# A fourth PSUM bank for two attention streams, taken from a third, and every engine's order laid out anew

## The reference

```
x = x + latent_attention(LN(x))      # low-rank keys/values, rotation of 16-wide heads, softmax
x = x + head_mixing(LN(x), ctx)      # per token, 16 heads of width 64 attend to the 16 heads of ctx
x = x + routed_ffn(LN(x))            # the 128 best tokens go through gelu(h W1 + b1) W2 + b2
x = x + sparse_attention(LN(x))      # of each row of scores the 25 largest are kept, the others set to 0, softmax
x = x + context_attention(LN(x), ctx, lens)   # keys past a sample's length are masked
x = x + linear(LN(x), ternary(weight))
```

## Time and profile before

| | |
|---|---|
| time, median of 3 runs | 6425.71 us (6419.53 to 6441.65) |
| the profiled execution's own time | 6419.66 us |
| its span, first to last instruction | 6417.9 us |
| busy share PE, PEld, DVE, ACT, POOL | 89%, 59%, 70%, 62%, 23% |
| mean granted TensorE clock | 0.914 of full |
| matmul records | 37476 |
| a double pass in the loop | 382.2 us for most |

### The profile page before, as it was taken

How to read it: one execution, slowest core, us unless ns; L and a number is a source line. 1 busy time by engine, 2 the same in 40 slices (tenths; PEclk the granted TensorE clock), 3 DMA queues, 4 the chain that set the end, 5 groups by cost and what they waited for, 6 DMA issues and landing times. The chain is left out here.

```text
span 6417.9 us, 109223 instructions
## 1 busy us (share of the span) xinstructions
PE 5732.7 (89%) x37476; PEld 3762.5 (59%) x37762; DVE 4510.0 (70%) x16186; ACT 4001.4 (62%) x9761; POOL 1506.5 (23%) x2564
## 2 busy tenths in 40 slices
PE   6799899899998999899899998999899899998875
PEld 3566566566556666556566555666556566556542
DVE  1476777677776677777677776777787767777763
ACT  2566666666676666676666676666676656676642
POOL 0122222122222222222222222222222222222220
PEclk7898999999999999999989999999999989999975
DMA  2000000000000000000000000000000000000000
GB/s 83 4 3 8 8 8 6 6 8 5 8 6 10 4 8 4 8 8 6 6 8 5 8 6 10 4 8 4 8 8 6 10 4 5 8 6 8 4 4 4
DMA packets 29373, 53.28 MB, mean 8 GB/s; under 512 B 8146, under 2 KB 9811, under 8 KB 27987
## 3 DMA queue, kind: packets, MB, share of 16 engines
q1 hardware_dynamic: 28770, 45.73, 2.2%
HBM read 37.33 MB, written 8.39 MB: 7 GB/s over the span
## 5 line engine op out<-in xcount | busy, mean ns | idle before, releaser
L972 POOL TENSOR_TENSOR t_pr<-t_pr,sc 128x512 f32<-128x512 f32 x512 | 650.6, 1271 | 1554.3 <-ACT t_pr L896 1553.8
L404 DVE TENSOR_REDUCE m_nm<-bankM 128x2 f32<-128x512 f32 x1024 | 669.0, 682 | 454.9 <-PE bankM L394 454.6
L945 DVE MATCH_REPLACE8 wk<-m,wk 128x256 f32<-128x256 f32 x2048 | 819.8, 407 | 0.0
L941 DVE MAX8 m<-wk 128x8 f32<-128x256 f32 x2048 | 756.3, 410 | 0.0
L448 PE MATMUL bankM<-m_q,m_kT 32*128 32x512 f32 x2048 | 685.6, 750 | 0.0
L394 PE MATMUL bankM<-m_kT,m_q 32*128 32x256 f32 x4096 | 613.7, 419 | 35.5 <-DVE m_nm L404 28.2
L902 ACT ACTIVATE t_pr<-t_pr,t_nm 128x256 f32<-128x256 f32 x1024 | 463.8, 502 | 264.5 <-POOL t_pr L972 260.3
L707 ACT ACTIVATE xk_area<-bankH,xb 64x256 f32<-64x256 f32 x1024 | 479.3, 468 | 125.5 <-PE bankH L602 106.9
L462 ACT ACTIVATE m_pT<-bankM,keymask 128x512 f32<-128x512 f32 x512 | 323.7, 683 | 314.6 <-PE bankM L448 313.9
L966 POOL TENSOR_SCALAR mx<-m 128x2 f32<-128x2 f32 x512 | 115.4, 225 | 1705.9 <-DVE wk L945 1702.9
L394 PEld LDWEIGHTS bankM<-m_kT,m_q 32*128 32x128 f32 x4096 | 369.4, 193 | 230.1 <-issue 145.7
(11 more groups left out here) (207 smaller groups left out, 11627.9 us busy)
## 6 DMA issues: line engine op xcount, KB each, us to landing
xin<-x_in SPq DMA_DIRECT2D x32, 256.0 KB, 2.7
ctxA<-ctx_in SPq DMA_DIRECT2D x32, 256.0 KB, 2.9
ctxB<-ctx_in SPq DMA_DIRECT2D x32, 256.0 KB, 2.7
out<-x SPq DMA_DIRECT2D x32, 256.0 KB, 2.0
w<-w_w SPq DMA_DIRECT2D x2, 1024.0 KB
xwq<-w_xwq SPq DMA_DIRECT2D x1, 1024.0 KB
xwk<-w_xwk SPq DMA_DIRECT2D x1, 1024.0 KB
xwv<-w_xwv SPq DMA_DIRECT2D x1, 1024.0 KB
```

What stands on the lines that cost most here:

```text
L404: nc.vector.tensor_reduce(b["nm"][:, i % 2, 2 * (i // 2) + x, :], banks[u % 3][:].rearrange("p (j s) -> p j s", j=2), AX.X, ALU.max, negat ...
L941: link.inc(nc.vector.max(top, src[:, t, :]))
L945: m = nc.vector.match_replace(out=wk[:, k, t, :], in_to_replace=take, in_values=src[:, t, :], imm_value=-BIG)
L972: nc.gpsimd.tensor_tensor(sp_[:, u % 2], taken[:, u % 2], sc[:, u % 3], ALU.mult).then_inc(g["sp_mul"], 1)
```

## The change

bankM gets four banks and bankH two.

- Score steps of m and c go through four banks (2i and 2i+1 mod 4), and step i waits for max 2i-2; steps 0 and 1 do not wait for a max. The maxima read bank u mod 4.
- Transposed score steps go through bankM 0, 1 and 3 in turns of one bank instead of two: step i waits for 2i-1 exps instead of 2i (step 1 for one).
- Stream h has one list TURNS of its 17 early steps (12 projections, LN transposes, four value transposes), which take turns on the two banks, each waiting for the eviction two turns back. By the list all four query projections fall on bank 1, the LN and value transposes on 0 and 1: v0 0, v1 1, v2 0, ln 1, v3 0, q0 1, t0 0, q1 1, t1 0, q2 1, t2 0, q3 1, t3 0, k0 1, k1 0, k2 1, k3 0.
- All quad scores use bankH 0, and quad s waits for the exps of quad s-1 (before: s-2). Bank 1 has what bank 2 had. FFN steps are renumbered alike; the second layer's first four steps wait for four gelus at once.
- Both tables are new for all four engines. The number of loop rounds stays 14.

No instruction of a compute engine is added or taken away.

```diff
-        bankT, bankM, bankH = banks("bankT", 2), banks("bankM", 3), banks("bankH", 3)
+        bankT, bankM, bankH = banks("bankT", 2), banks("bankM", 4), banks("bankH", 2)
...
         def at_scores_T(pe, n, b, bank, i):
             m, c = i // 2, i % 2
+            bank = [bank[(0, 1, 3)[(2 * i + x) % 3]] for x in range(2)]
             yield
             if i == 0:
                 pe.wait_ge(*at(g[n + "_m3"], 1))
+            elif i >= 2:
+                pe.wait_ge(*at(g[n + "_ex"], 2 * i - 1))
             else:
-                pe.wait_ge(*at(g[n + "_ex"], 2 * i))
+                pe.wait_ge(*at(g[n + "_ex"], 1))
...
-                else:
-                    pe.wait_ge(*at(g[n + "_nm"], max(1, 2 * i - 1)))
-                at_scores(n, b, [bankM[2 * i % 3], bankM[(2 * i + 1) % 3]], i, masked)
+                elif i >= 2:
+                    pe.wait_ge(*at(g[n + "_nm"], 2 * i - 2))
+                at_scores(n, b, [bankM[2 * i % 4], bankM[(2 * i + 1) % 4]], i, masked)
...
+        TURNS = ["v0", "v1", "v2", "ln", "v3", "q0", "t0", "q1", "t1", "q2", "t2", "q3", "t3", "k0", "k1", "k2", "k3"]
+            for n, what in enumerate(TURNS):
+                bank = bankH[n % 2]
+                yield
...
+                if n >= 2:
+                    pe.wait_ge(*at(*turn_read(n - 2)))
...
                 if s < QUADS:
                     yield
                     if s == 0:
                         pe.wait_ge(*at(g["hm_ev"], 48))
-                    if s >= 2:
-                        pe.wait_ge(*at(g["hm_ex"], 4 * (s - 1)))
+                    if s >= 1:
+                        pe.wait_ge(*at(g["hm_ex"], 4 * s))
                     for i in range(4):
                         c = 4 * s + i
-                        last = nc.tensor.matmul(bankH[s % 2][:, i * P:(i + 1) * P], xqT[:, c, :], xkT[:, c, :], start=True, stop=True)
+                        last = nc.tensor.matmul(bankH[0][:, i * P:(i + 1) * P], xqT[:, c, :], xkT[:, c, :], start=True, stop=True)
...
             for f in range(FF // P):
                 yield
-                pe.wait_ge(*at(g["md_hid"], f + 1))
+                pe.wait_ge(*at(g["md_hid"], max(4, f + 1)))
```

More of the change, by code:

```diff
@@ L97 @@
+        t7 h t c3 h m t2 m h t4 h2 t6 m t2 h t h c t4 h t5 h t"""),
 }
@@ L588, in tensor_h @@
         def tensor_h(pe):
-            for k in range(12):
-                which, quad = k // 4, k % 4
+            for n, what in enumerate(TURNS):
+                bank = bankH[n % 2]
                 yield
-                if k == 0:
+                if n == 0:
                     past(pe, "md_x3", "ctxA_in")
[L594 to L599, removed]
-                    for d in range(ND):
[L601 to L612, removed]
@@ new lines, in tensor_h @@
+                if n >= 2:
+                    pe.wait_ge(*at(*turn_read(n - 2)))
+                if what == "ln":
+                    pe.wait_ge(*at(g["ln1_xn"], 2))
+                    for d in range(ND):
+                        for t in range(NT):
+                            last = nc.tensor.transpose(bank[:, d * S + t * P:d * S + (t + 1) * P],
+                                                       lnH["xn"][:, t, d * P:(d + 1) * P], w["ident"][:])
+                    last.then_inc(g["ln1_tr"], 1)
+                elif what[0] == "t":
+                    v = int(what[1])
+                    if v == 0:
+                        pe.wait_ge(*at(g["hm_ev"], 16))
@@ L613, in tensor_h @@
                     for i in range(8):
-                        last = nc.tensor.transpose(bankH[2][:, i * XD:(i + 1) * XD], xvT[:, v * 8 + i, :], w["ident"][0:XD, 0:XD])
+                        last = nc.tensor.transpose(bank[:, i * XD:(i + 1) * XD], xvT[:, v * 8 + i, :], w["ident"][0:XD, 0:XD])
                     last.then_inc(g["hm_vtr"], 1)
+                else:
+                    quad = int(what[1])
+                    if what == "q0":
+                        pe.wait_ge(*at(g["ln1_xT"], 1))
+                    wt, src = {"v": ("xwv", ctxA), "q": ("xwq", lnH["xT"]), "k": ("xwk", ctxA)}[what[0]]
+                    for hp in range(2):
+                        for d in range(ND):
+                            c = (quad * 2 + hp) * P
+                            last = nc.tensor.matmul(bank[:, hp * S:(hp + 1) * S], w[wt][:, d, c:c + P], src[:, d, :],
+                                                    start=(d == 0), stop=(d == ND - 1))
+                    last.then_inc(g["hm_proj"], 1)
@@ L659, in tensor_h @@
             for d in range(ND):
-                last = nc.tensor.matmul(bankH[2][:, 0:S], w["wrt"][:, d, :], lnH["xT"][:, d, :], start=(d == 0), stop=(d == ND - 1))
+                last = nc.tensor.matmul(bankH[0][:, 0:S], w["wrt"][:, d, :], lnH["xT"][:, d, :], start=(d == 0), stop=(d == ND - 1))
             last.then_inc(g["md_sps"], 1)
@@ L669, in tensor_h @@
             for t in range(NT):
-                last = nc.tensor.transpose(bankH[1][:, t * P:(t + 1) * P], pick[:, t, :], w["ident"][:])
+                last = nc.tensor.transpose(bankH[0][:, t * P:(t + 1) * P], pick[:, t, :], w["ident"][:])
             last.then_inc(g["md_ptr"], 1)
@@ L691, in tensor_h @@
             for t in range(NT):
-                last = nc.tensor.matmul(bankH[2][:, t * D:(t + 1) * D], pickT[:, t, :], yff[:], start=True, stop=True)
+                last = nc.tensor.matmul(bankH[0][:, t * D:(t + 1) * D], pickT[:, t, :], yff[:], start=True, stop=True)
             last.then_inc(g["md_u"], 1)
```

102 lines of the change are left out of this document (54 added, 48 removed).

## The result

The changed kernel took 6501.2 us (median of 4 runs, 6471.0 to 6538.7), the kernel before on the same chip 6422.6: ratio 1.0126 [1.0069, 1.0182]. A second set of 7 runs on another chip gave 6542.0 us and 1.0191 [1.0157, 1.0224]. The forecast was 6305 us in a range of 6215 to 6465, with a chance of 0.23 for slower.

A forecast was written before the change was run, and what follows sets the result against it. PE was taken to bound the loop, losing time to waits and half-clock stretches. From 6419.7 us, -20 (end passes), -35 (loop waits) and -60 (clock) gave 6305 us; own range 6270 to 6340, range of all cases 6215 to 6465.

The forecast's parts named there:

- Fourth bank, ends: Single-stream first and last pass and the four between: M's bank waits go, together -20 us, bounds -8 and -35.
- deducted 3 us: Four passes between the ends: 6 us gained from the fourth M bank, less 3 for the tighter h.
- my slower rival: Single quad bank: each lap's seven quad waits for the previous exps 0.5 us late, +105 us, 6470 us; chance 0.23.
- Loop waits: Per double pass: 8.7 us of waits removed, 6.4 added, net -2.3; -35 us over about 15 double passes.
- The choice: Lap's end: token choice after t's last round, and gelu's start behind m.onT, add 1.7 us per lap, 3.4 per double pass.
- h.s0 in lap 2: PE's wait for key evictions ahead of h's first quad in lap 2: 2.8 us where it was 2.1.
- LN5: c's LN5 follows a t round and a quad maximum on DVE: +0.8 us per lap, 1.6 per double pass.
- t.tr3, 0.75 us: Lap 1: about 0.75 us of wait ahead of this t transpose, its exps behind two key evictions on ACT.
- Clock: Lap 1's 20.5 us fall stays away in about half of the double passes: 7.5 x 8 = -60 us.
- nothing like 3.5 us idle in 10.5: Walk through lap 1: largest waits 0.75, 0.5 and 0.45 us, so its clock fall, 8 us, may not come.
- The rule that I set aside: Bank waits themselves feed the clock falls, so removing them should help in both laps: -120 us in place of -60.
- What the forecast named as fatal: Forecast wrong if mean clock stays at 0.914, or PE waits several us for the token choice at each lap's end.

The follow-up runs named there:

- Experiments 4: Kernel before with four idle matmuls each behind the shift-row and h.s0 waits: 6579.1 us, 1.021; one more ahead of m's score steps 1 and 2: 0.9779.
- 6: t's second and third selection rounds over half the columns: kernel before 0.9801, with idle matmuls 0.9587; changed kernel 0.992, with them 0.9723, or with t earlier instead 1.0091.
- Experiments 2: Changed kernel with h's token choice on VectorE moved behind the first round of t's last head, not its last round: 6525.6 us, 1.0176.

## Why the forecast failed, by its steps

- **Fourth bank, ends: -20 forecast, -8 measured (1053 to 1045), of which -3 in the single pass, which the forecast had counted with the loop.** The bank waits went nearly as said, and the low clock fell with them, for which I had counted nothing (by 7 us in the first pass and by 19 in the last): first pass 114.0 to 104.4 us, last 102.5 to 87.3. But the pass with m and h alone went from 134.4 to 154.3, for which I had deducted 3 us: PE is idle 34.8 us there instead of 24.8, and the low clock is 69 instead of 38. There no t or c covers the two-bank H. Of its waits (PE's in that pass, changed kernel) the last is the one that my slower rival described (0.6 us before); the other two are turns on the two banks by transposes of probabilities (3.7 before) and by projections (none before):

```profile
PE bankH L646 <- ACT xot L756: 6.8, 4, 1.7
...
PE bankH L633 <- ACT xq_area L727: 5.0, 4, 1.4
PE bankH L656 <- ACT xp L749: 4.6, 2, 2.3
```

- **Loop waits: -2.3 forecast, +7.4 and +7.9 of idle time and +4 to 5 us of length measured.** Removed were 5.4 and not 8.7: exps went from 4.5 to 2.8, maxima from 1.2 to 0.4, and the copies of shift rows and layer norm from 4.4 to 1.5. Added were some 12 and not 6.4. The choice was sized about right (3.7 against 3.4), and h.s0 in lap 2 came out at 2.7 (forecast 2.8); LN5 was oversized (the waits for layer norms grew by 0.4, forecast 1.6). The failed term is t: I had followed one transpose (t.tr3, 0.75 us) and not the others, and six of them wait for 5.9 us in all and six value steps for 3.0.
- **Clock: -60 forecast, +74 and -18 in the two profiles (63.4 and 48.8 us of low clock against 51.7, at 0.45 over 14 passes).** With the waits this step turned the sign. Long falls did go, from 1.93 per double pass to 1.29 and 0.86, but those of lap 2 (13 to 6 and 5), not those of lap 1 (10 to 12 and 7), which I had named; the 4 behind m's score steps went too. Yet with the waits that the order adds come short falls (which wait goes with which fall isn't shown), 1.4 per pass before and 5.4 to 6.2 now, mostly of 3.4 to 6.8 us, and the falls left in lap 1 last up to 30.7 us instead of up to 20.5. I had weighed each wait by its length, looked for the few of over 1 us, and taken "nothing like 3.5 us idle in 10.5" for safety.
- **The rule that I set aside.** The Trainium skill, "TensorE: Matmul & The Clock Gate", section "A second HAM failure mode: psum-queue depth-cycling", tells of a kernel whose short idle gaps between groups of matmuls, while it cycles through PSUM banks, made the clock swing. I held against it that bank waits of 0.6 in m's phase are followed by no fall. That was read from one pass and is wrong for the trace as a whole: 4 of the 27 long falls of before, of 27.3 us each, begin right behind m's waits for maxima of 0.2 and 0.4 us. One of them (PE in order of time, then the stretches before the fall and in it):

```profile
2065.35 1.13 PE L394 MATMUL bankM<-m_kT,m_q 32*128 32x256 f32 x8 [0.18 <-DVE m_nm L404]
2066.41 1.16 PE L636 MATMUL bankH<-xk_area,xq_area 72*128 72x128 f32 x8
2067.99 1.54 PE L394 MATMUL bankM<-m_kT,m_q 32*128 32x256 f32 x8 [0.41 <-DVE m_nm L404]
...
2058.10:2068.60 10.50, 9.72 (x67) 6.92 (x67) 10.50 (x41) 7.93 (x18) 3.45 (x5) 1.00 0.10 28
2068.60:2095.90 27.30, 26.66 (x130) 17.01 (x127) 18.92 (x59) 9.46 (x28) 5.99 (x13) 0.50 0.00 1
```

Experiments 4 and 6 agree with the page: without m's bank waits of 0.2 to 0.5 us, 26 long falls in 14 passes went in the one and 7 in the other. But the same waits were followed by no long fall in 24 of 28 laps of before, so by themselves they do not bring one.

- **The slower rival, 0.23.** The sign was its own, the place was not: in the loop no quad waits for its predecessor's exps. What the forecast named as fatal did occur: the clock did not rise from 0.914, and PE waits for the choice at each lap's end, 2.6 and 1.6 us. Experiments 2 and 6 show that this wait alone was not the loss.
- Left open: why the same program position falls in some passes and not in others (those of one execution differ by 82 us of low clock), and which of the order's steps makes t's transposes late.

## What to carry to other kernels

Where the granted clock has low stretches, read the length of each loop pass against its low-clock time first; the slope (here 0.45) prices the clock apart from the waits. Then look at the thin phases in which TensorE pauses often and briefly, and try a few idle matmuls there, one place at a time: ten per lap gave 3.7% here, most fills elsewhere gave nothing or cost. Count falls over all passes and not in one, and compare executions of equal mean clock: two profiles of the same changed kernel lie 76 us apart. And when an order is planned afresh, list every wait it adds, small ones too, on the stream that was not the subject of the change.

## What the hardware showed that I had not expected

- The same instructions, with PE idle for nearly the same time (40.0 and 38.0 us), ran a double pass in 375 and in 406 us in one execution.
- Idle time ahead of a fall does not rank places: 3.5 us in 10.5, 1.5 in 10.5 and 1.0 in 9.5 were each followed by 20 to 31 us at clock 0.50.
- The spread between executions goes with the clock too: 93 us (6183 to 6276, clock 0.956 to 0.940) with long falls in some passes, 19 us (6185 to 6204) with none. It is no rule: with t earlier there was no long fall either, and the executions lie 44 us apart.
